# A smaller lag of the layer-norm and router rows behind attention, and a second PSUM bank for the last two rows' router scores

## What is computed

```
x = layernorm(x + self_attention(x))            # 16 heads of 16, causal      ("phase D")
x = layernorm(x + cross_attention(x, ctx, ctx)) # 16 heads of 16, causal      ("phase E")
x = layernorm(x + moe(x))   # 8 experts, top 2, router scores = x @ Wr,
                            # plus a shared SwiGLU gated by sigmoid(x @ Wsg)   ("phase F")
```

## Time and profile before

| | us |
|---|---|
| median of 3 runs | 779.85 (777.71 to 783.6) |
| the profiled execution | 774.44 |
| its span, first to last instruction | 772.3 |
| PE / DVE / ACT busy | 672.7 / 559.9 / 489.1 |
| POOL busy | 250.7 |
| matmuls of `values` (L1905) | 127.6 |
| exps (L937) | 150.0 |
| softmax (L1373, without the reads of its accumulator) | 132.8 |

### The profile page before, as it was taken

The page is one execution under the profiler, slowest core; times in us unless marked ns, Lnnn a source line. Parts: engine busy times, 40 slices in busy tenths (PEclk is TensorE's granted clock), DMA queues, the critical chain, the costliest instruction groups (busy, mean ns, idle before and its releaser), DMA issues.

```text
span 772.3 us, 18597 instructions
## 1 busy us (share of the span) xinstructions
PE 672.7 (87%) x4914; PEld 603.0 (78%) x4915; DVE 559.9 (73%) x2515; ACT 489.1 (63%) x1354; POOL 250.7 (32%) x422
## 2 busy tenths in 40 slices
PE   5899799777774988999999999997799989999982
PEld 5788577634443988999999899996799978888881
DVE  4788588767887547888888999996857565555386
ACT  4456566458771328899999999994355545555443
POOL 4443200223335400122212122223164405555454
PEclk9999899958875999999999999998899999999996
DMA  9950000000003685667766766641044523333162
GB/s 287 359 153 0 1 1 1 1 0 2 0 1 109 186 287 188 194 201 209 215 198 192 194 202 172 163 132 45 15 130 128 165 62 100 97 103 101 48 228 81
DMA packets 66489, 95.61 MB, mean 124 GB/s; under 512 B 11390, under 2 KB 52992, under 8 KB 66304
## 3 DMA queue, kind: packets, MB, share of 16 engines
q1 hardware_dynamic: 63024, 86.51, 37.9%
q0 software_dynamic: 3408, 8.43, 3.1%
HBM read 62.45 MB, written 33.36 MB: 124 GB/s over the span
## 4 chain that ended last, share of the span: by engine, by line
PE 43%; issue 17%; DVE 17%; SPq 9%; ACT 6%; DMA 4%; POOL 2%; DVEq 0%; ACTq 0%; POOLq 0%
PE bank L1905 8%; PE bank L2047 5%; PE bank L1981 5%; SPq L494 5%; PE bank L1891 5%; PE bank L1637 4%; PE bank L2071 3%; PE bank L1998 3%; SPq L490 3%; PE bank L1880 2%; PE bank L2035 2%; PE bank L1921 1%; DVE X L1119 1%; PE bank L2056 1%; POOL rstd L613 1%
## 5 line engine op out<-in xcount | busy, mean ns | idle before, releaser
L937 ACT ACTIVATE late_mem<-bank,smax 128x128 f32<-128x128 f32 x512 | 150.0, 404 | 14.7 <-DVE smax L1373 13.0
L1373 DVE CUSTOM_DVE_ANT_0 bank<-bank,causal 128x128 f32<-128x128 f32 x512 | 132.8, 323 | 18.1 <-issue 16.9
L1905 PE MATMUL bank<-f_mem,late_mem 128*128 128x68 f32 (+3 forms) x1024 | 127.6, 267 | 0.0
L1905 PEld LDWEIGHTS bank<-f_mem,late_mem 128*128 128x128 f32 x1024 | 124.3, 192 | 0.4 <-issue 0.4
L613 POOL TENSOR_TENSOR rstd<-var,power 128x2 f32<-128x2 f32 (+1 forms) x64 | 40.3, 629 | 194.6 <-DVE var L1112 183.7
L947 ACT ACTIVATE late_mem<-bank 128x512 f32<-128x512 f32 x128 | 81.7, 638 | 4.0 <-PE bank L1891 3.1
L1891 PE MATMUL bank<-ident,late_mem 128*128 128x128 f32 x512 | 78.7, 277 | 3.3 <-ACT late_mem L937 3.0
L1373 DVE DVE_READ_ACCUMULATOR2_ANT smax<- 128x1 f32 x512 | 72.5, 142 | 0.0
L1880 PE MATMUL bank<-kz,qs 128*128 128x256 f32 x256 | 63.6, 331 | 3.9 <-DMA kz<-k_E 2.9
L1891 PEld LDWEIGHTS bank<-ident,late_mem 128*128 128x128 f32 x512 | 59.4, 142 | 5.9 <-ACT late_mem L937 5.7
L1981 PE MATMUL bank<-x_hi,w_hi 128*128 128x256 f32 x176 | 51.3, 291 | 1.0 <-DVE x_lo L1431 1.0
(11 more groups left out here) (283 smaller groups left out, 2003.6 us busy)
## 6 DMA issues: line engine op xcount, KB each, us to landing
qs<-q_D SPq DMA_DIRECT2D x64, 128.0 KB, 2.7
kz<-k_D SPq DMA_DIRECT2D x128, 64.0 KB, 2.6
qs<-q_E SPq DMA_DIRECT2D x64, 128.0 KB, 2.8
kz<-k_E SPq DMA_DIRECT2D x128, 64.0 KB, 2.5
xg<-f_mem SPq DMA_DIRECT2D x1, 5031.0 KB, 22.4
late_mem<-xg SPq DMA_DIRECT2D x39, 129.0 KB
q_D<-stage_d SPq DMA_DIRECT2D x8, 512.0 KB, 2.9
k_D<-stage_d SPq DMA_DIRECT2D x8, 512.0 KB, 4.0
```

What stands on the lines that cost most here:

```text
L937: ins = sc.activation(sp[:, g, i, :], bank[g][:, i * P:(i + 1) * P], ACT.Exp, bias=smax[:, g, i:i + 1], scale=-1.0)
L1373: ins = ve.tensor_tensor_reduce(v[:, i, :], v[:, i, :], causal[:, :], -1.0, 3e38, ALU.add, ALU.min, smax[:, g, i:i + 1])
L1905: ins = mm(bank[6][:, h * (DH + 1):to * (DH + 1)], spt[:, g, i, :], vf[:, slot, h:to, :].rearrange("p h d -> p (h d)"), start=True, stop=True)
```

## The change

Rows of D are transposed with a lag of 4 turns and rows of E with a lag of 3 (before 5 for both). The statistics, inverse root, apply and copy steps move with them: D at 3, E at 2. Inside a turn, xpose_row("D") moves behind the xpose_out of group 1, and e_high moves behind the exps of group 1 and evac_ot. e_low keeps its place on DVE. The router scores of rows 14 and 15 go to bank 3 instead of bank 7, and the waits on F_score are changed to suit.

```diff
-LAG_XP = 5
+LAG_XP = 4
+LAG_XE = 3
...
+        def score_bank(t):
+            return bank[NG - 1] if isinstance(t, int) and t > B - LAG_XE else bank[7]
...
-            pipelined_pair(pool, B, [(LAG_XP + 1, None, keep_xt), (0, values("D", V), values("E", CTX)),
-                                     (3, inverse_root("D", 1), inverse_root("E", 1)),
-                                     (4, copy_row("D"), copy_row("E"))])
+            pipelined_pair(pool, B, [(LAG_XE + 1, None, keep_xt), (0, values("D", V), values("E", CTX)),
+                                     (3, inverse_root("D", 1), None), (2, None, inverse_root("E", 1)),
+                                     (3, copy_row("D"), None), (2, None, copy_row("E"))])
...
                 if g == 0:
-                    stages += [(LAG_XP, e_high, None), (2, None, w_high)]
+                    stages.append((2, None, w_high))
                 if g == 1:
-                    stages += [(2, evac_ot, None), (LAG_XP, None, f_xt)]
+                    stages += [(2, evac_ot, None), (LAG_XP, e_high, None), (LAG_XE, None, f_xt)]
...
-                ve.tensor_copy(score[:, bass.ds(t, 1), :], bank[7][:, 0:E + 1].unsqueeze(1)
+                ve.tensor_copy(score[:, bass.ds(t, 1), :], score_bank(t)[:, 0:E + 1].unsqueeze(1)
...
-            pipelined_pair(dve, B, [(LAG_XP + 1, None, f_scores), both(0, 0, softmax), (3, d_stats, e_stats),
-                                    both(1, 0, softmax), (LAG_XP, e_low, None), both(2, 0, softmax),
-                                    (4, d_apply, e_apply), both(3, 0, softmax), (1, heads_out("D"), heads_out("E")),
+            pipelined_pair(dve, B, [(LAG_XE + 1, None, f_scores), both(0, 0, softmax), (3, d_stats, None),
+                                    (2, None, e_stats), both(1, 0, softmax), (LAG_XP, e_low, None), both(2, 0, softmax),
+                                    (3, d_apply, None), (2, None, e_apply), both(3, 0, softmax),
+                                    (1, heads_out("D"), heads_out("E")),
                                     (2, None, w_low)])
...
-                            pe.wait_ge(sem("F_score"), t)
+                            pe.wait_ge(sem("F_score"), min(t, B - LAG_XE + 1) if isinstance(t, int) else t)
...
                 pe.wait_ge(sem("F_xt"), t + 1)
+                if isinstance(t, int) and t > B - LAG_XE + 1:
+                    pe.wait_ge(sem("F_score"), t)
                 for c in range(KC):
-                    ins = mm(bank[7][:, 0:E + 1], xt1[:, slot, c, :], r1[:, c, :], start=(c == 0), stop=(c == KC - 1))
+                    ins = mm(score_bank(t)[:, 0:E + 1], xt1[:, slot, c, :], r1[:, c, :], start=(c == 0), stop=(c == KC - 1))
...
-                if g == 0:
-                    stages.append((LAG_XP, xpose_row("D"), None))
                 if g == 1:
-                    stages += [(2, xpose_out, None), (LAG_XP, None, xpose_row("E"))]
-            stages += [(2, project, None), (LAG_XP, None, f_router)]
+                    stages += [(2, xpose_out, None), (LAG_XP, xpose_row("D"), None), (LAG_XE, None, xpose_row("E"))]
+            stages += [(2, project, None), (LAG_XE, None, f_router)]
```

## The result

The changed kernel takes 791.45 us (median of 4 runs, 789.7 to 793.83), the kernel before 780.58 us beside it (4 runs, 777.71 to 783.6): 1.0161 times as long, interval 1.0117 to 1.0205. The forecast was slower by 2.4%, 798.6 us, with a range of 789 to 806; the sign is right, the time lies in the range, and the size is 7 us too large.

What follows compares the result with a forecast made beforehand. The prediction took PE to bound phase D, with DVE close behind. Its terms, +23.9 - 0.9 + 0.3 - 4.5 = +18.8 us, added to the median 779.85, gave 798.6 us, range 789 to 806.

Steps and rivals of the forecast that it cites:

- PE is early everywhere: In phase D's longer loop, PE's work is ready before needed; PE idles some 1.45 us a turn before group 3's scores.
- Part 1, e_high and e_low: In phase D, e_low waits on DVE for the later e_high; turns of 8.94 us against 7.49, +23.9 us in all.
- DVE's 0.49 us of idle time, nothing else: In a phase D turn, only this DVE slack hides any of e_low's 1.93 us delay.
- Turns 18 and 19: Last turns with e_low: two rows' statistics and apply +1.65 us, w_low +0.4, missing evac_ot -0.5.
- Part 2, PE's place: Moving xpose_row in D behind group 1 on PE gains nothing and can't cost: 0, bounds -0.2 to +0.2 us a turn.
- Part 3, E's rows: At the end of attention, E's lag of 3 leaves three rows instead of five: -4.5 us, bounds -3.5 to -6.5.
- The step about the second bank: At the end of attention, bank 3 lets row 15's transpose precede row 14's score copy; without it, up to 1 us less.
- The release: When e_low's loop ends, DVE makes good most of the reciprocal's 1.1 us lag beside PE: about -0.9 us.
- The basis: Whole kernel: the change of +18.8 us is added to the timed median 779.85, 5.4 above the profiled execution.
- Only the end moves: Rival: ACT reaches e_high before DVE comes to e_low, nothing waits, 4.2 us gained: 775.7 us; chance 0.04.
- The stacks hide a part: Rival: SP's issue of stacks bounds turns 14 to 19, so 8.7 us of the loss vanish: 789.9 us; chance 0.08.
- PE's clock falls in phase D: Rival: PE's idling brings half clock in three of sixteen turns, +18 us: 817 us; chance 0.06.

Runs made afterwards that it cites:

- ACT's place alone: Kernel after with only PE's xpose_row(D) put back to the end of group 0; e_high stays behind group 1's exps and evac_ot: 791.34 us, ratio 1.0163.
- the last group: Ten timed runs of the kernel before, unchanged, repeated for a second profile: median 782.25 us, ratio 1.0007.
- both places undone: Kernel after with xpose_row(D) and e_high put back to their old places, small lags and second score bank kept: 771.76 us, ratio 0.9898.
- the two places alone: Kernel before with only xpose_row(D) and e_high moved to their new places, lag 5 and one score bank kept: 796.45 us, ratio 1.0197.

## Why the prediction was right, and where it was off

**What bounds the kernel.** Right: PE at full clock, DVE close behind. "PE is early everywhere" in the new loop was wrong by a little. The scores of group 0 start 0.23 us behind the reciprocal (352.97), and DVE waits 0.15 us at 353.60, 0.04 us behind their end.

**Part 1, e_high and e_low.** The mechanism and each of its steps came out: evac_ot, e_high, e_low and softmax 0.26, 0.45 and 0.35 us apart (forecast 0.26, 0.47 and 0.35), a DVE wait of 1.75 us (forecast 1.9) in the steady turns with e_low, and a PE wait of 0.85 us ahead of group 3's scores (forecast 1.4). The experiment with ACT's place alone has the whole loss. What failed is the size: "DVE's 0.49 us of idle time, nothing else". That was the labelled wait of the earlier trace rows. The timeline of before holds two more gaps without a label, visible only as steps between starts: group 2's softmax to group 3's is 346.34 - 344.85 = 1.49 us (344.85 from the earlier trace rows), after 1.29; group 3's to the reciprocal 347.57 - 346.34 = 1.23, after 0.96. These are 0.20 + 0.27 = 0.47 us more of slack. With the 0.15 us of waiting for PE that stay, the turn is 8.94 - 0.47 + 0.15 = 8.62, measured 8.60. The two further starts of before, from its timeline:

```profile
346.34 0.29 DVE L1373 CUSTOM_DVE_ANT_0 bank<-bank,causal 128x128 f32<-128x128 f32 x1
...
347.57 0.26 DVE L1382 RECIPROCAL rden<-bank 128x16 f32<-128x16 f32 x1
```

The lower bound of the term, 1.3 us a turn, had counted 0.13 us of this as possibly idle, and the measured 1.11 lies below it. One rule, fitted to these turns, holds for every kernel in which e_low's time is all that holds up DVE: the turn is the larger of 7.49 and 6.69 + the delay of e_low. It gives 7.49 and 7.66 for delays of 0.59 and 0.97 (measured 7.49, 7.65), 8.31 for the 349.95 - 347.37 - 0.96 = 1.62 us of the kernel with e_high ahead of evac_ot (8.32), and 8.59 for the 1.90 of the kernel after (8.60). In turns 4 to 17 the miss is 14 x 8.94 = 125.2 against 120.87 us: -4.3.

**Turns 18 and 19.** Forecast 19.43, measured 19.46, but not by the reasons given. Turn 18 lasts 9.88 us (forecast 8.94 + 1.65 - 0.25 = 10.3) and turn 19 9.58 (9.1), in which the granted clock is 0.50 to 0.65. In the kernel with e_high ahead of evac_ot the clock stays at 1.00 there and turn 19 takes 8.38 us. So the agreement of the sum is luck: a turn 18 that was forecast too long, and a fallen clock that this term didn't have. The prediction also placed PE's waits for stacks in turns 16 to 18; in the profile of before the two that fall into turns 4 to 19 stand in turns 18 (0.46 us) and 19 (1.40).

**Part 2, PE's place.** 0 as forecast in this change, where e_high is late anyway. The argument for it was too general: "it can't cost" looked at PE's own queue and at POOL and SP, and left out the reader of the transpose. With e_high at its old place ACT waits 1.09 us for it, and the turn grows by 0.53.

**Part 3, E's rows.** Right: forecast -4.5, measured -4.39, and the first FFN matmul stands 7.23 us behind the last reciprocal (forecast 7.1). The step about the second bank failed: "what lets row 15's transpose go", "up to 1 us less" without it. It is 0.

**The rest.** The release, forecast at -0.9 + 0.3, came to -0.16. The 2.24 us behind the first FFN matmul were not forecast. That part took 228.7 to 234.7 us in the profiles of all these kernels, and 229.8 and 234.7 in two of the same kernel, so no cause in the change is needed for it. It goes with the clock: the same 1442 matmuls keep PE busy for 199.65 us at a mean granted clock of 0.95 in the first profile of before, for 204.27 at 0.93 in the second, and for 202.59 at 0.93 in the profile after.

**The basis.** In the profiles the terms sum to +17.3 us against +18.8, and that they are so near is partly luck: the 4.3 us too many in turns 4 to 17 are offset by the 2.24 us of the FFN and by 0.4 us of the release. The larger part of the 7 us is another step: "the three timed runs have a median of 779.85, 5.4 above it; on this basis". The profiled execution of before was among its shorter ones: other groups of runs of this kernel have medians of 778.11 to 782.25. Its second profile is longer, by one turn with a fallen clock and in the FFN. The kernel after was profiled at its median (791.32 and 791.45). A difference between an untypically short execution of before and an ordinary one of after is not the difference of the medians: the medians differ by 10.9 us, the profiled executions by 16.9. That the ordinary execution of before contains a turn with a fallen clock, as its second profile does, would explain a part. The mean granted clock of the timed runs, 0.917 to 0.925 in the longer ones of the last group, points the same way; where in those runs it fell was not measured.

**The rivals.** Only the end moves: it needs a kernel in which e_high comes in time, and that is the experiment with e_high ahead of the exps of group 1, 775.51 us. That this is so near the rival's 775.7 is luck: the kernel before beside it had a median of 781.75, not 779.85. The stacks hide a part: turns 14 to 17 take 8.55 to 8.62 us like the others, so no. PE's clock falls in phase D: it keeps 1.00 from 325 to 390 us, with PE idle 6.1 us there, 0.8 us a turn. But one sign that the prediction named as wrong did show, a clock below 1.00 before 460 us: 0.50 and 0.65 from 448 to 456 us, in turn 19 alone. It cost some 1 to 1.5 us (last section) and not the 18 us of the rival. The Trainium skill, "TensorE: Matmul & The Clock Gate" ("A second HAM failure mode: psum-queue depth-cycling"), has short pauses between groups of matmuls make the clock swing; the turns from 325 to 390 us don't agree with it, with 58.88 of 65 us busy at 1.00. Where the clock did fall in the kernel after, PE had waited 2.05 us at 446.17, in a stretch with 1.95 of 4 us busy; the same wait left it at 1.00 in two other kernels (last section).

## What to carry to other kernels

A step that stands on one engine behind work which itself waits for the consumer's engine turns two parallel streams into a series: follow the moved instruction's new predecessors back to the engine that will wait for it. Slack is not the labelled waits alone; take the same steps' starts in a stretch where they are known to run back to back, and call the difference slack, or put in small dummy instructions and see from which delay on the turn grows. A move on the producer's side is priced at its reader, and a forecast made from a profile is compared with the medians only after asking whether that profile was a typical one.

## What the runs showed of the hardware that was not expected

The granted clock fell at the passage from phase D to E in some profiles and not in others, behind the same idling of PE. Two stretches in which it did not fall, with the one that follows (columns as above), of the kernel with e_high ahead of evac_ot and of the first profile of before:

```profile
440.00:444.00 4.00, 1.96 (x18) 1.85 (x17) 2.46 (x21) 1.90 (x6) 0.54 (x1) 1.00 0.60 168
444.00:448.00 4.00, 3.54 (x30) 3.13 (x29) 3.93 (x27) 3.51 (x12) 1.43 (x3) 1.00 0.62 184
```

```profile
428.00:432.00 4.00, 2.60 (x24) 2.53 (x24) 3.37 (x21) 3.95 (x14) 1.03 (x2) 1.00 0.66 176
432.00:436.00 4.00, 4.00 (x38) 4.00 (x38) 3.51 (x26) 3.02 (x9) 0.54 (x1) 1.00 0.84 233
```

Beside them stand stretches just as idle with a fall behind them. The kernel after has 1.95 of 4 us busy and then 0.50, the kernel with ACT's place alone 1.96 and then 0.62, and the second profile of before 2.59 and then 0.66. With e_low behind the softmax of group 2 there are again 1.97 of 4 us busy and no fall; PE's wait in it is 2.04 us, as long as in the kernel after. With both places undone the clock falls to 0.59 behind a stretch with 3.22 of 4 us busy, in which no wait of PE is longer than 0.39 us. So these profiles don't tell from PE's idling whether the clock falls, and what decides it isn't shown.

The price is read from turns with the same instructions. Turn 19 takes 9.58 and 9.41 us with a fallen clock (the kernel after, ACT's place alone) and 8.38 and 8.12 without (e_high ahead of evac_ot, whose steady turn is 0.28 us shorter, and e_low behind group 2). Turn 21 takes 11.12 us in the kernel with the two places alone, at 0.68, 0.50 and 0.54 from 464 to 476 us, against 7.21 in the first profile of before: 3.9 us. In the second profile of before it takes 9.59, 2.4 us more than 7.21, and a part of that may be the stack that came later (a wait of 1.37 us against 0.60). Pauses of 0.8 us in every turn of 8.6, over fourteen turns, cost no clock at all: it is 1.00 from 317 to 444 us in the kernel after. And two executions of one program, with the same steady turns, can have spans 7.9 us apart (772.3 and 780.2).
